# The start lags of three PE row groups in a gated two-convolution kernel: from 0, 6 and 12 units to 0, 4 and 8

## The reference

```python
def qconv_cg(x, w, theta):                 # base = 64 // 4 = 16 channels
    yp = conv3x3(x[:, :base], w[:, :base])
    yr = conv3x3(x[:, base:], w[:, base:])
    d = jax.nn.sigmoid(2.0 * (yp - theta[None, :, None, None]))
    return yp + d * yr
h = jax.nn.relu(bn(qconv_cg(x, w_a, theta_a), gamma_a, beta_a, mean_a, var_a))
h = bn(qconv_cg(h, w_b, theta_b), gamma_b, beta_b, mean_b, var_b)
return jax.nn.relu(x + h)
```

## Time and profile before

| | |
|---|---|
| median of 3 runs | 440.07 us (439.25 to 441.33) |
| the profiled execution | 439.4 us, of which the span from first to last instruction is 437.5 us |
| mean granted TensorE clock of the span | 0.994 |
| PE busy | 427.3 us, 98% of the span |
| DVE busy, ACT busy | 245.1 us (56%), 197.2 us (45%) |
| HBM traffic | 13.60 MB read, 12.85 MB written |

### The profile page before, as it was taken

One profiled execution on the slowest core, in us unless ns is written; L12 is line 12 of the kernel. 1 busy time (PEld: TensorE's weight loads), 2 busy tenths in 40 slices (PEclk: granted clock), 3 DMA queues, 4 the chain that ended last, 5 costly groups with the idle time before them and its releaser, 6 DMA issues.

```text
span 437.5 us, 17328 instructions
## 1 busy us (share of the span) xinstructions
PE 427.3 (98%) x7826; PEld 423.9 (97%) x7826; DVE 245.1 (56%) x414; ACT 197.2 (45%) x340; POOL 32.2 (7%) x82
## 2 busy tenths in 40 slices
PE   7999999999999999999999999999999999999992
PEld 6999999999999999999999999999999999999992
DVE  6566546744754862574475476366457457536624
ACT  6755344534534652453353453354345344424223
POOL 6221000000000100000000000011000000000001
PEclk9999999999999999999999999999999999999997
DMA  8920026142426110410523241161622422012044
GB/s 170 190 62 4 3 49 122 35 92 51 88 37 124 25 27 2 99 43 11 124 50 75 49 98 41 37 120 26 121 49 51 76 49 49 3 27 51 14 86 92
DMA packets 119530, 27.57 MB, mean 63 GB/s; under 512 B 119328, under 2 KB 119328, under 8 KB 119456
## 3 DMA queue, kind: packets, MB, share of 16 engines
q1 hardware_dynamic: 117488, 26.09, 29.8%
q10 hardware_dynamic: 1648, 0.36, 0.4%
q0 software_dynamic: 320, 0.00, 0.0%
HBM read 13.60 MB, written 12.85 MB: 60 GB/s over the span
## 4 chain that ended last, share of the span: by engine, by line
PE 96%; ACT 1%; DMA 1%; DVE 0%; ACTq 0%; issue 0%
PE acc L511 96%; DMA early<-in_L_conv_w_a_dram 1%; ACT rows_out L678 0%; PE acc L457 0%; ACT L631 0%; DVE early L718 0%; ACT w_hi L601 0%; ACTq L354 0%; ACT mix L653 0%; ACT z L661 0%; ACT rows_out L676 0%; ACT x_hi L621 0%; ACT probe L631 0%; PE acc L544 0%; ACTq L600 0%
## 5 line engine op out<-in xcount | busy, mean ns | idle before, releaser
L511 PE MATMUL acc<-x_hi,w_hi 32*128 32x456 f32 (+1 forms) x1392 | 278.5, 358 | 0.4 <-ACT x_hi L621 0.4
L511 PE MATMUL acc<-x_lo,w_hi 32*128 32x456 f32 (+1 forms) x1392 | 278.9, 358 | 0.0
L511 PE MATMUL acc<-x_hi,w_lo 32*128 32x456 f32 (+1 forms) x1392 | 278.6, 359 | 0.0
L511 PE MATMUL acc<-h_hi,w_hi 32*128 32x512 f32 x1152 | 263.5, 389 | 0.0
L511 PE MATMUL acc<-h_hi,w_lo 32*128 32x512 f32 x1152 | 263.3, 389 | 0.0
L511 PE MATMUL acc<-h_lo,w_hi 32*128 32x512 f32 x1152 | 263.3, 389 | 0.0
L511 PEld LDWEIGHTS acc<-x_hi,w_lo 32*128 32x128 f32 x1392 | 235.6, 183 | 0.3
L511 PEld LDWEIGHTS acc<-x_lo,w_hi 32*128 32x128 f32 x1392 | 235.7, 183 | 0.1
L511 PEld LDWEIGHTS acc<-x_hi,w_hi 32*128 32x128 f32 x1392 | 234.6, 183 | 1.1 <-ACT x_hi L621 0.8
L511 PEld LDWEIGHTS acc<-h_hi,w_hi 32*128 32x128 f32 x1152 | 200.3, 183 | 0.0
L511 PEld LDWEIGHTS acc<-h_lo,w_hi 32*128 32x128 f32 x1152 | 198.7, 183 | 0.0
(11 more groups left out here) (78 smaller groups left out, 179.4 us busy)
## 6 DMA issues: line engine op xcount, KB each, us to landing
out_dram<-rows_out SPq DMA_DIRECT2D x95, 126.0 KB, 2.7
x<-in_x_dram SPq DMA_DIRECT2D x28, 392.0 KB, 5.5
x<-in_x_dram SPq DMA_DIRECT2D x2, 294.0 KB, 4.3
x<-in_x_dram SPq DMA_DIRECT2D x2, 280.0 KB, 4.9
early<-in_x_dram SPq DMA_DIRECT2D x4, 112.0 KB, 4.1
out_dram<-rows_out SPq DMA_DIRECT2D x3, 112.0 KB, 2.4
x<-in_x_dram SPq DMA_DIRECT2D x2, 98.0 KB, 3.9
early<-in_L_conv_w_a_dram SPq DMA_DIRECT2D x1, 144.0 KB, 3.1
```

What stands on the lines that cost most here:

```text
L511: return pe.matmul(sums(bank, blk), w[g * ROWS:(g + 1) * ROWS, tap], moving(blk, part, c, dx, g), start=(u == 0 and (alone or g == bank_gr ...
```

## The change

One constant changes. Group 2 begins its visits at step 18 v + 4 in place of 18 v + 6, and group 3 at 18 v + 8 in place of 18 v + 12. Group 1 stays at 18 v, group 0 at 18 v + 6. The spare matmuls of the start go from 6 to 4 for group 2 and from 12 to 8 for group 3.

```diff
 ROUND = len(TURNS)
-OFFSET = (6, 0, 6, 12)
+OFFSET = (6, 0, 4, 8)
 EARLY = 3
```

## The result

The changed kernel takes 441.31 us (median of 14 runs), the kernel before 439.38 in the same series. The ratio is 1.0032 with a 95% interval of 1.0020 to 1.0044: 1.4 us slower, 0.9 to 1.9. (The two medians lie 1.9 us apart, since the times of the kernel before fall into three clusters, 8 at 439.1 to 439.4 us, 3 at 440.1 to 440.3 and 3 at 441.3 to 441.5, and its median into the lowest.) That is within the 0.5% that the prediction called no change, and inside its range, but about twice the 0.75 us of its sum.

A forecast was written before the change was run, and what follows sets the result against it. The prediction took each row group's own series of PE matmuls as the bound. 0.36 (start) + 0.4 (hand-overs) + 0 (banks) + 0 (end), about 0.75 us, took the median from 440.07 to 440.8 us, range 439.2 to 442.6.

The forecast's parts named there:

- Groups run at their own pace: PE's steady part: each row group starts matmuls at its own width's pace; its series of 1944 units bounds, whatever the offsets.
- rival 3: PE's whole order: groups march in step, 1952 steps in place of 1956, a gain of 1.1 us; chance 0.09 with rival 4.
- Two units left undone at the start: PE's queue stops at step 4 for the second x_hi chunk; groups 1 and 0 have two units less done, 0.36 us.
- The last gate: ACT's gate of the last block, a sign of being right: some 0.4 to 0.8 us later than 428.50.
- What is behind the stop: After the start's stop: does anything swallow the loss? The parameter chain moves along, so all 0.36 us, bounds 0 and 0.36.
- The hand-overs: Waits for yr banks, eight a round: at lag 4 drift between groups meets them in early rounds, 0.4 us, bounds 0 and 0.9.
- rival 1: Bank hand-overs: release and reload cost more than 0.55 us, deciding from 0.84 on; at 0.95 the time is 446; chance 0.07.
- Reuse of the banks: A round's third block begins 4 units earlier; its bank's slack falls from 1.59 to some 0.75 us, cost 0.
- rival 2: Third block's bank isn't free: `gated` 0.1 us later than the slack allows in most rounds, 2.5 us, 443.3; chance 0.04.
- The end: Kernel's tail: group 3 finishes 0.83 us earlier but the chain leaves PE with group 0, so 0, bounds -0.83 and 0.
- Rival 4: Kernel's tail: group 3 sets the end after all, -0.83 us, 439.3; chance 0.09 together with rival 3.
- rival 5: Start and hand-overs: the gap hides the shift of two units and no hand-over binds, 440.1; chance 0.08.

The follow-up runs named there:

- e12_fill_look: The changed kernel with four spare matmuls per row group put before the wait for the second x_hi chunk, second profile: 439.73 us.
- e8_look: The changed kernel with no edit, profiled a third time: 441.35 us.
- e4_lag8: The kernel before with groups 2 and 3 at offsets 8 and 16 in place of 6 and 12: 445.56 us, ratio 1.0133.
- e9_g0: The kernel before with group 0's offset 0 in place of 6: 438.88 us, ratio 0.9979.
- e7_before_move: The kernel before with ACT's table load for the square root moved behind the first three x_hi chunks: ratio 0.9997.

## Why the prediction was right or wrong

*Groups run at their own pace, so offsets don't shorten the series*: right. The long piece is 410.36 against 410.25 us over some 1,900 units of each group, and rival 3 (in step, 1.1 us gained) didn't happen.

*Two units left undone at the start, 0.36 us*: right where it can be seen by itself. With the clock held in both, e12_fill_look reaches the steady part 0.30 us later than the kernel before. Counted from the restart behind the stop, 8.59 in the earlier trace rows and here

```profile
8.54 0.45 PE L512 MATMUL acc<-x_hi,w_hi 32*128 32x398 f32 x2
```

it takes 9.98 against 9.63 us, 0.35 more. The last gate, which was to come 0.4 to 0.8 us later than 428.50, comes at 428.90 there; in the profile after, with its late clock, it comes at 431.19.

*What is behind the stop*: this is the step that failed. The prediction asked what might swallow the 0.36 us, and found nothing, but took PE's pace at the start as given. The stop at step 4 is longer (0.80 us idle against the 0.41 in the earlier trace rows) and comes after fewer matmuls, and where the full clock was granted early, it can fall behind the stop. That was worth 1.61 us between e8_look and e12_fill_look. It is the missing term of the sum: 0.30 and 0.11 are in it, the other 1.0 of the 1.4 us isn't. (The 1.0 is a mean over executions with a fall and without; no run measures it by itself.) The Trainium skill, "TensorE: Matmul & The Clock Gate", Part 1, "What's actually happening", has the lower clock as the default state, which activity lifts; e8_look and e12_fill_look agree, 0.50 and 1.00 behind the same wait.

*The hand-overs, 0 to 0.9, taken as 0.4 us*: the mechanism was right, the size too large. It measured 0.11 us (410.36 in all six profiles with lags of 4 and 8 from the start and group 0 at 6, 410.25 in all three with 6 and 12). It arises where the prediction put it: counted from the start of the long piece, group 0's visits end no more than 0.05 us later than before up to the eighth, 0.16 by the twelfth, in the rounds that mix 398 and 512, and no later after that. That a wait holds them there no row shows directly at lag 4; at lag 2 (e4_lag8) it does, and rival 1 needs that lag.

*Reuse of the banks, 0*: right, 0.77 us of slack against some 0.75; rival 2 is out.

*The end, 0*: right. From the last gate to the last ReLU it took 3.82 us both times, though group 3 came earlier; e9_g0 shows from the other side that group 0 set the end. Rival 4 is out, and rival 5 too.

*The number*: nearer than the sum deserved, by luck. 440.8 stands on a base of 440.07, the median of 3 runs, one from each cluster. On 439.38, the median of the 14 runs in the series of the result, the same sum gives 440.1, below all 14 times of the changed kernel. So a base 0.7 us too high, and a term for the hand-overs 0.3 us too large, made up for the clock that wasn't in the sum.

Open: in some executions the full clock comes only at 10 us or later (10.96 and 13.09 in the changed kernel, 10.36 in e7_before_move, where the start is that of the kernel before but for the table load). How often, and whether the change makes it come later still in those, a few profiles can't tell. Nor is it settled what makes the clock fall, the length of the stop or the fewer matmuls ahead of it: the spare matmuls change both, and the move of the table load left at least 3 falls in 12 executions, with a stop of unknown length.

## What to carry to other kernels

An order written out by hand has a start of its own: list for each early wait how much work stands ahead of it in the queue, and what the producer's time is. Where PE stands still in the first microseconds, price the stop by the clock too, and try to fill it, with units of the real work if the order can have them there. And before shortening the lag of one group, look which group the end of the chain leaves PE with.

## What the runs showed of the hardware

A stop of PE of 0.80 us, at 7.8 to 8.6 us, was followed by the fall of the granted clock from full to half, which then lasted from 8.62 to 12.03 (e8_look); with 0.41 us of idle time and more matmuls ahead of it (profile before) it didn't fall. By the mean granted clock it fell in at least 5, perhaps 10, of 21 executions of the changed kernel (0.985 to 0.991), while none of 75 of the kernel before is below 0.992. The steady part repeats to 0.01 us between executions: 410.25 or 410.36, by the lags, in nine profiles with starts of 18.2 to 20.9 us. And row groups of PE, fed from one queue, drift against each other, by up to some 0.7 us or 3 units in the profile before, without loss until a wait in that queue holds all: with 2 units between hand-overs that cost 0.2 us a round, with 4 it was 0.11 us in all.
